# A unit's negated row maxima: one transpose of 32 columns and rows of 256 bytes, in place of four transposes and rows of 1024 bytes

## What is computed

```python
k_eff = (W_dq.T @ W_uq.T @ W_uk).reshape(nh, hs, n_kvl)        # 16 heads, hs = 8, n_kvl = 64
q_lat = einsum('bqhd,hdl->bhql', q, k_eff)
attn  = einsum('bhql,bkl->bhqk', q_lat, c_kv) / sqrt(hs)        # causal
attn  = softmax(where(causal, attn, -inf))
y     = (attn @ c_kv) @ v_eff
x     = layernorm(x + y)
# mixture of experts: 2 groups of 1024 tokens, 8 experts of width 512, top 2, 80 places each
x     = layernorm(x + moe(x))
```

## Time and profile before

| | |
|---|---|
| timed runs, median (lowest to highest) | 597.27 us (596.22 to 597.64) |
| the profiled execution: its own time | 596.03 us |
| its span, first to last instruction | 594.3 us |
| TensorE matmuls, busy | 526.7 us, 89% of the span |
| VectorE, busy | 447.7 us, 75% |
| ScalarE, busy | 347.2 us, 58% |
| GpSimd, busy | 63.1 us, 11% |
| all DMA | 25410 packets, 24.90 MB |

### The profile page before, as it was taken

How to read it: one execution, slowest core, us unless ns; L and a number is a source line. 1 busy time by engine, 2 the same in 40 slices (tenths; PEclk the granted TensorE clock), 3 DMA queues, 4 the chain that set the end, 5 groups by cost and what they waited for, 6 DMA issues and landing times.

```text
span 594.3 us, 10315 instructions
## 1 busy us (share of the span) xinstructions
PE 526.7 (89%) x3491; PEld 217.0 (37%) x3491; DVE 447.7 (75%) x1311; ACT 347.2 (58%) x711; POOL 63.1 (11%) x64
## 2 busy tenths in 40 slices
PE   4967999889999998989989999989999999946990
PEld 2523333333333333224445333333233332232890
DVE  3786999898888988866757878978879852448516
ACT  0614556656667765755755767667777779920230
POOL 9400000000000000540000550000000000000040
PEclk9966999999999999998999999999999999976996
DMA  3489893200000300110000260000000000000024
GB/s 86 124 216 206 209 274 81 43 2 2 2 2 1 82 2 2 36 59 1 2 12 1 44 42 0 2 2 1 1 2 2 1 2 10 28 1 1 11 35 49
DMA packets 25410, 24.90 MB, mean 42 GB/s; under 512 B 2314, under 2 KB 22668, under 8 KB 25356
## 3 DMA queue, kind: packets, MB, share of 16 engines
q1 hardware_dynamic: 21660, 20.42, 14.0%
q0 software_dynamic: 1280, 2.62, 3.7%
q10 hardware_dynamic: 2416, 1.18, 0.7%
HBM read 16.81 MB, written 7.28 MB: 41 GB/s over the span
## 4 chain that ended last, share of the span: by engine, by line
PE 57%; issue 20%; DVE 13%; DMA 3%; POOL 3%; ACT 2%; SPq 0%; ACTq 0%; DVEq 0%; POOLq 0%
PE acc L1078 16%; PE ring L1039 15%; PE ring L1061 14%; POOL exp_in L565 2%; DVE part_max L768 2%; DVE unused L773 2%; PE ring L1065 2%; DMA qT<-maxT 1%; PE ms L1169 1%; PE ms L1163 1%; DVE kT L928 1%; PE ring L1169 1%; PE ring L1163 1%; DVE stats L802 1%; DMA wo<-in_L_attn_W_dkv 1%
## 5 line engine op out<-in xcount | busy, mean ns | idle before, releaser
L648 ACT ACTIVATE probs<-ring 128x512 f32<-128x512 f32 (+3 forms) x560 | 268.4, 537 | 137.9 <-PE ring L1065 74.8
L768 DVE TENSOR_REDUCE part_max<-ring 128x1 f32<-128x512 f32 x384 | 254.3, 685 | 46.8 <-PE ring L1039 44.0
L1039 PE MATMUL ring<-kT,qT 126*128 126x512 bf16 (+3 forms) x640 | 221.9, 361 | 10.3 <-DVE part_max L773 4.5
L1061 PE MATMUL ring<-qT,kT 128*128 128x512 bf16 (+3 forms) x640 | 214.7, 352 | 3.8 <-DMA qT<-maxT 3.5
L1078 PE MATMUL acc<-probs,v 128*9 128x512 f32 (+3 forms) x1280 | 147.7, 534 | 0.9 <-ACT yT L659 0.9
L773 DVE CUSTOM_DVE_ANT_0 unused<-ring,causal 128x128 bf16<-128x128 f32 (+3 forms) x256 | 120.1, 483 | 21.8 <-PE ring L1039 19.6
L1039 PEld LDWEIGHTS ring<-kT,qT 126*128 126x128 bf16 x640 | 62.0, 98 | 178.5 <-DVE part_max L768 102.3
L1061 PEld LDWEIGHTS ring<-qT,kT 128*128 128x128 bf16 x640 | 61.9, 99 | 47.2 <-ACT probs L646 15.7
L1065 PE MATMUL ring<-later,ident 128*128 128x128 bf16 x256 | 55.4, 221 | 0.0
L1078 PEld LDWEIGHTS acc<-probs,v 128*9 128x9 f32 x1280 | 19.0, 88 | 50.6 <-issue 25.9
L646 ACT ACTIVATE probs<-ring 128x1024 f32<-128x1024 f32 (+3 forms) x40 | 33.2, 898 | 3.1 <-issue 1.8
(11 more groups left out here) (174 smaller groups left out, 340.3 us busy)
## 6 DMA issues: line engine op xcount, KB each, us to landing
kT<-parts_k SPq DMA_DIRECT2D x9, 384.0 KB
qT<-parts_q SPq DMA_DIRECT2D x9, 384.0 KB
wi<-in_L_ffn_wi SPq DMA_DIRECT2D x1, 2048.0 KB, 18.7
parts_k<-wi SPq DMA_DIRECT2D x3, 384.0 KB, 4.0
parts_q<-wi SPq DMA_DIRECT2D x3, 384.0 KB, 4.8
kT<-parts_k SPq DMA_DIRECT2D x12, 96.0 KB
qT<-parts_q SPq DMA_DIRECT2D x12, 96.0 KB
x<-in_L_attn_x ACTq DMA_DIRECT2D x4, 256.0 KB, 4.1
```

What stands on the lines that cost most here:

```text
L648: nc.scalar.activation(probs[:, at, 0:width], ring[:, bank, 0:width], ACT.Exp).then_inc(exp_done, 1)
L768: nc.vector.tensor_reduce(dst, sc[i % SRING][:, :], AX.X, ALU.max).then_inc(sc_used, 1)
L1039: nc.tensor.matmul(sc[i % SRING][:, 0:w], qT[s % 2][0:MROW, head, qt * P:(qt + 1) * P], kT[0:MROW, head, c * QUERIES:c * QUERIES + w], sta ...
L1061: ins = nc.tensor.matmul(bank[:, 0:QUERIES - off], kT[:, head, j * P:(j + 1) * P], qT[s % 2][:, head, off:QUERIES], start=True, stop=True, ...
```

## The change

The 32 columns of `max16` change their order, from (query tile, part, head) to (part, head, query tile). One transpose turns all 32 at once, into 32 partitions of 128 columns. `maxT` becomes 32 x 128, and the DMA's 8 KB go in 32 runs of 256 bytes, since 128 queries of one head and part now lie on one partition. The work on VectorE keeps its instructions and their sizes.

```diff
-        max16 = [sb(f"max16_{i}", [P, QT, 2, HG], BF16) for i in range(2)]
-        maxT = [sb(f"maxT{i}", [2 * HG, QUERIES], BF16) for i in range(2)]
+        max16 = [sb(f"max16_{i}", [P, 2, HG, QT], BF16) for i in range(2)]
+        maxT = [sb(f"maxT{i}", [2 * HG * QT, P], BF16) for i in range(2)]
...
-                nc.scalar.activation(maxT[u % 2][:, :], bank.bitcast(BF16)[0:2 * HG, 0:QUERIES], ACT.Copy).then_inc(maxT_kept, 1)
+                nc.scalar.activation(maxT[u % 2][:, :], bank.bitcast(BF16)[0:2 * HG * QT, 0:P], ACT.Copy).then_inc(maxT_kept, 1)
...
-                act.dma_start(qT[super_of(u) % 2][MROW:MROW + 2, g * HG:(g + 1) * HG, :], maxT[u % 2][:, :]).then_inc(max_in[u % 2], 16)
+                rows = qT[super_of(u) % 2][MROW:MROW + 2, g * HG:(g + 1) * HG, :]
+                act.dma_start(rows.rearrange("a h (q t) -> a h q t", t=P), maxT[u % 2][:, :]).then_inc(max_in[u % 2], 16)
...
-                nm = neg_max[:, :].rearrange("p (q h) -> p q h", q=QT)
-                link(nc.vector.tensor_copy(m[:, :, 0, :], nm))
-                nc.vector.tensor_tensor(m[:, :, 1, :], nm, m[:, :, 0, :], ALU.subtract).then_inc(max_done, 1)
+                nm = neg_max[:, :].rearrange("p (q h) -> p h q", q=QT)
+                link(nc.vector.tensor_copy(m[:, 0, :, :], nm))
+                nc.vector.tensor_tensor(m[:, 1, :, :], nm, m[:, 0, :, :], ALU.subtract).then_inc(max_done, 1)
...
-                for q in range(QT):
-                    ins = nc.tensor.transpose(bank.bitcast(BF16)[0:2 * HG, q * P:(q + 1) * P],
-                                              max16[u % 2][:, q, :, :].rearrange("p a h -> p (a h)"), ident16[:, :])
-                return ins
+                return nc.tensor.transpose(bank.bitcast(BF16)[0:2 * HG * QT, 0:P],
+                                           max16[u % 2][:, :, :, :].rearrange("p a h q -> p (a h q)"), ident16[:, :])
```

## The result

Over 20 timed runs of each kernel, the change has a median of 592.18 us against 595.21: a ratio of 0.9951, 95% interval 0.993 to 0.9973. That is 2.9 us faster, between 1.6 and 4.2. (One of the change's 20 runs took 1714.78 us and one of E5's twelve 686.36, disturbances that the comparisons leave out.) The same kernel measured once more, beside other runs of before (596.6), had 592.17 and a ratio of 0.9922 [0.9905, 0.9939]: 4.7 us, between 3.6 and 5.7. The change's own median repeats within 0.01 us; before's moves by over a microsecond from one set of runs to the next. A single execution can't be read finely, then: before's 20 lie between 591.51 and 597.64 us, the change's between 589.30 and 594.69. The lowest differ by 2.2 us, the highest by 2.9.

What follows compares the result with a forecast made beforehand. TensorE was taken as the limit from 90 us, shared with VectorE from 55, with unit 0's transfer holding up the start. Turns 2.3 plus units 0 and 1 net 1.6 gave 3.9 us off 597.27: 593.4 us, range 591.5 to 596.9.

Steps and rivals of the forecast that it cites:

- The sixteen turns: One transpose per unit instead of four saves 0.17 us of TensorE; with the copy's part 2.3 us, bounds 1.3 and 3.5.
- units 5 and 11: Next turn wants the same bank, so the copy's length counts: 0.6 us together, bounds 0.3 and 1.0.
- Unit 10: Its turn lies ahead of TensorE's 2.86 us wait for the experts' inputs, so its saving was put at 0.
- units 1 to 4: Where VectorE is as full as TensorE, the turns save between 0 and 0.7 us; 0.3 taken.
- units 6, 7, 8, 9: With units 12 to 15, where TensorE is the limit: 8 x 0.17 = 1.4 us saved.
- The copy: ScalarE's copy from PSUM, 578 ns, loses 0.32 us; worth 0.6 us behind units 5 and 11, nothing in other units.
- Unit 0's transfer: when.: Issue moves from 40.76 to 40.17, one backlog place earlier: packets at 45.55 instead of 48.13; 2.58 us, bounds 0 and 2.58.
- Unit 0's transfer: how long.: Sixteen 256-byte rows per engine instead of four of 1024 lengthen unit 0's run by 0.2 us, bounds 0 and 0.9.
- twice both under load: Unit 0's run, 0.26 us against 0.20 in the quiet, taken as about double for both on loaded engines.
- What is late next.: Unit 1's rows then cause a new wait of 0 to 1.8 us, 0.8 taken; net of units 0 and 1, 1.6 us.
- The sum: 2.3 us from the turns plus 1.6 net from units 0 and 1: 3.9 us off, median 593.4 us.
- The rival that the place stays: Unit 0's rows keep their backlog place and lose 0.2 us, turns keep 2.3: 2.1 us off, 595.2 us; chance 0.22.

Runs made afterwards that it cites:

- E5: The change, with each unit's one transpose issued four times into the same place; 593.11 us, ratio 0.9952 to before.
- E6: The change, with ScalarE's 32 x 128 copy made twice, once into a tile nobody reads; 593.08 us, ratio 0.9955 to before.
- E4: The change, with unit 0's rows alone sent from GpSimd's queue instead of ScalarE's; 592.45 us, ratio 0.9958 to before.
- E12: The change measured once more without any edit, for a second profile; 592.17 us, ratio 0.9922 to before.
- E2: The change, with SyncE's six 384 KB loads for super 1 held until unit 0's rows have landed; 590.82 us, ratio 0.9928 to before.
- E3: The kernel before, with SyncE's six 384 KB loads for super 1 held until unit 0's rows have landed; 593.62 us, ratio 0.9976.
- E7: The change, with SyncE's super 1 loads held from the second on until unit 0's maxima are copied; 589.64 us, ratio 0.9909 to before.
- E8: The change, with SyncE's super 1 loads held from the third on until unit 0's rows have landed; 590.16 us, ratio 0.9918 to before.
- E1: The kernel before, with maxT padded so its rows go in 256-byte runs, transposes and copy unchanged; 596.65 us, ratio 1.0032.
- E11: E10 with E7's hold added; 586.0 us, ratio 0.9816 to before.
- E9: The kernel before, with group 0's experts' inputs turned two steps later; 590.11 us, ratio 0.9905.
- E10: The change, with group 0's experts' inputs turned two steps later; 587.32 us, ratio 0.9835 to before.

## Why the prediction was right or wrong

The direction and the time held: 593.4 us was forecast, 592.18 measured, and the forecast ratio of 0.9935 (593.4 / 597.27) lies inside the interval. The way there did not hold, in its larger single term, so that the time came out so near is in part luck: the terms as measured give 1.6 us, the forecast was 3.9, and the rest of the 2.9 measured has no cause shown.

- **The sixteen turns.** Right in mechanism, too high in size: 1.7 to 1.8 us in both profiles against 2.3. Units 6, 7, 8, 12 to 15 gave 0.14 to 0.17 each, as worked out, and so did E5 the other way round; units 5 and 11 gave 0.31 each. Unit 10 gave nothing, as foreseen. Mis-sized were units 1 to 4, at 0.3: nothing in either profile, VectorE sets the pace there. And unit 9, counted among "units 6, 7, 8, 9": its 0.17 us are given back within four microseconds. Half of it goes into the next wait for VectorE's row maxima, which is 0.62 us before (223.65) and 0.70 with the change (224.18).
- **The copy.** 253 ns against 0.26 estimated, and worth 0.31 in exactly two places. E6 shows that it is worth nothing elsewhere.
- **"Unit 0's transfer: when." This step failed.** It took the order of three issues for a rule: the second load done by 48.13 and the rows running just then, so a place in the backlog had to be worth 2.58 us and to be had by an issue 0.59 us earlier. Its reading of the earlier trace rows was already wrong. Twelve ends more don't mean that one load has just been done, since the engines don't end it together. The packets of the same row say how far they were: 5815 by 48.13, of which 4736 are super 0's and two belong to other queues, or 90 per engine beyond super 0. Most of the third load had run by then, and the rows did not run ahead of it. The issue did come 0.6 us earlier against its turn; the place was not to be had. The rows came behind 63 to 78 packets on each engine, 5.4 to 6.2 us of them from the end of the issue, on another queue (E4) and with an issue at 39.94 as well (E12). With less ahead they came sooner (E2, E3, E7, E8).
- **"Unit 0's transfer: how long."** 0.2 us were set aside, bounds 0 to 0.9; by the lengths of the runs it measured 0.6 to 1.3 (1.47 to 1.73 against 0.42 to 0.9), past the upper bound in some executions, and 0.5 at the first scores in E1, which has nothing else. The price of the packet was right (0.0175 against 0.0165 taken) and the step still missed: "twice both under load" was too little where a row took 0.1 us. That a packet of SyncE's passes between two rows fits those executions, but not E7 and E11.
- **"What is late next."** It didn't come up, as the first step wasn't earlier. Where it was (E2, E3, E7, E8), unit 1 waited 0.8 to 1.7 us, within the 0 to 1.8 given.
- **The sum.** 2.3 + 1.6 = 3.9 was forecast; the profiles account for 1.7 by the turns less 0.1 that is left of unit 0's loss at unit 4, so about 1.6. The rival that the place stays, 2.1 us, is what happened in kind; its 595.2 is above what was measured.
- **What stays open.** Measured were 2.9 us (1.6 to 4.2), and 4.7 (3.6 to 5.7) in the second comparison. The lowest runs, which should be those with the fewest falls of the clock, are 2.2 us apart. Over 1 us is missing. It may lie in the falls of the clock at 263 us: before and E1 lost 3.0 us each there, the change and its variants without a hold 1.5, 1.5, 1.6, 1.7 and 3.3 (the change, E4, E6, E5, E12), a mean of 1.9. That would be 1.1 us. But a timed run has no profile, seven profiles are few, and why the change should alter the fall isn't shown. What a timed run does have is its mean granted clock. Of the 67 runs of before beside the experiments 38 have 0.953 or 0.954, of the change's 25 in both sets five. At the same clock the change is still 2.3 to 2.5 us faster: 594.4 us against 596.8 at 0.953 and 0.954, 592.2 against 594.7 at 0.956, 590.9 against 593.3 at 0.958. So of the 3.2 us between the means of these runs some 0.8 go with a higher clock, and about 2.4 do not, of which the terms explain 1.6. Neither rest has a cause shown, and the mean counts the clock in waits too. E9 against E10 was meant to settle it and did not. It is open too why none of the four kernels with a hold (E2, E3, E7, E8) has a fall there, though their waits are as long (2.7 to 3.1 us) and only stand some 3 us earlier. With it, a part of the holds' gain in the timed runs may be the clock's and not unit 0's.

## What to carry to other kernels

A transfer issued into a loaded set of DMA engines can wait for what they already have in front of them, here 63 to 78 packets each and over 5 us, from ScalarE's queue and from GpSimd's alike: to have it earlier, hold back the large loads in front of it, and don't count on a slightly earlier issue; look next at who then waits. Check in the trace that the hold leaves ahead what it was meant to leave. Count the rows of a small transfer per engine under load, since sixteen took up to 1.7 us here, while in the quiet they are nearly free. Before you say which of several transfers is done, count all their packets, since the engines don't end one together. And before a gain of a few tenths per cent is judged, look for waits of 2 to 3 us on TensorE: the clock behind one cost 0, 1.5 or 3 us here, and moving the task that waits by two steps gave more than the change did (medians of 6.5 us against 3.0).

## What was not expected of the hardware

- The granted clock's fall behind a wait is not the same in every execution. The wait at 263 us, 2.7 to 3.6 us long, was followed by a stretch of four microseconds at 0.50 to 0.72 in seven profiles and by none in four, the four with a hold. Behind waits of 2.84 and 2.86 us the change lost 1.5 us and before 3.0. The wait of 1.93 us at 380 to 390 us, which all fourteen profiles have, was followed by 0.60 in E9, 0.57 in E11 and 1.00 in the other twelve.
- Rows of a small transfer are not always run in a block: 34 packets took 1.5 to 1.7 us beside SyncE's in most executions but 0.6 and 0.4 in E7 and E11, 0.43 with nothing behind (E8) and 0.25 in the quiet.
- A transfer of unit 0's size runs 1.4 us after its issue begins if no load is ahead (E2, E3), 5.2 to 5.8 with two loads of 384 KB ahead (E7, E8, E11), and 6.7 to 7.6 with the whole backlog.
- The 12 engines under one load don't end it together: in before the twelve ends that follow the first load's come one by one from 45.6 to 48.1 us.
